# Three of six moves inside SBUF as ScalarE copies in place of DMA transfers, in a non-local attention block

## The reference

```
theta = x' w_theta' + b_theta          (N x Ci)
phi   = w_phi x + b_phi                (Ci x N)
g     = x' w_g' + b_g                  (N x Ci)
att   = softmax(theta phi, over the last axis)      (N x N)
y     = att g                          (N x Ci)
out   = w_out y + b_out, then batch norm by given mean, variance, gamma and beta
result = x + out
```

## Time and profile before

| what | value |
|---|---|
| median of three runs | 206.3 us (206.23 to 206.87) |
| the profiled execution | 205.01 us, of which 203.2 us are the span |
| TensorE's granted clock, as a share of full | 0.997 |
| PE, PEld (weight loads) busy | 195.2 us, 133.6 us |
| DVE, ACT, POOL busy | 174.8 us, 136.8 us, 154.2 us |
| DMA: bytes moved, hardware queue q1 | 35.28 MB, 81.3% of 16 engines' span |

### The profile page before, as it was taken

How to read it: one execution, slowest core, us unless ns; L and a number is a source line. 1 busy time by engine, 2 the same in 40 slices (tenths; PEclk the granted TensorE clock), 3 DMA queues, 4 the chain that set the end, 5 groups by cost and what they waited for, 6 DMA issues and landing times.

```text
span 203.2 us, 3990 instructions
## 1 busy us (share of the span) xinstructions
PE 195.2 (96%) x1100; PEld 133.6 (66%) x1100; DVE 174.8 (86%) x289; ACT 136.8 (67%) x245; POOL 154.2 (76%) x130
## 2 busy tenths in 40 slices
PE   7998899999999999999999999999999998999993
PEld 7485776587666857677566957677566956566551
DVE  0687989988997899978998899978998899989881
ACT  2679867767486766866577765866577675767731
POOL 2479579999778999699987999699988964954300
PEclk9999999999999999999999999999999999999998
DMA  5309946799999998899979998899988998848102
GB/s 154 98 7 225 240 85 117 167 248 185 188 219 250 222 169 221 187 224 187 233 159 259 230 191 194 168 249 203 198 180 182 226 169 182 132 81 155 52 3 103
DMA packets 59500, 35.28 MB, mean 174 GB/s; under 512 B 50400, under 2 KB 50912, under 8 KB 59488
## 3 DMA queue, kind: packets, MB, share of 16 engines
q1 hardware_dynamic: 59200, 35.01, 81.3%
q10 hardware_dynamic: 288, 0.14, 0.2%
HBM read 8.36 MB, written 4.23 MB: 62 GB/s over the span
## 4 chain that ended last, share of the span: by engine, by line
PE 71%; DVE 10%; DMA 5%; POOL 5%; SPq 4%; issue 3%; ACT 1%; ACTq 0%; DVEq 0%; POOLq 0%
PE ps_scores L757 21%; PE ps_flip L821 12%; PE ps_y L769 11%; PE ps_misc L783 6%; PE ps_y L776 5%; PE ps_misc L741 5%; DVE neg_max L622 4%; PE ps_misc L864 4%; DMA pt_hi<-p_hi 3%; DVE pt_lo L663 3%; SPq L302 2%; POOL p_lo L478 2%; DMA w_tp<-w_tp_t_dram 2%; PE ps_scores L795 1%; POOL x_lo L492 1%
## 5 line engine op out<-in xcount | busy, mean ns | idle before, releaser
L552 ACT ACTIVATE probs<-ps_scores,neg_max 128x1024 f32<-128x1024 f32 x64 | 71.7, 1120 | 29.1 <-DVE neg_max L627 14.9
L622 DVE TENSOR_REDUCE neg_max<-ps_scores 128x1 f32<-128x1024 f32 x64 | 77.9, 1217 | 9.5 <-PE ps_scores L757 9.1
L663 DVE SCALAR_TENSOR_TENSOR pt_lo<-ps_flip,pt_hi 128x512 f16<-128x512 f32 x84 | 54.0, 684 | 5.2 <-ACT pt_hi L539 5.1
L539 ACT ACTIVATE pt_hi<-ps_flip 128x512 f16<-128x512 f32 x84 | 45.6, 595 | 15.2 <-PE ps_flip L821 15.2
L478 POOL TENSOR_TENSOR p_lo<-probs,p_hi 128x1024 f16<-128x1024 f32 x22 | 47.0, 2139 | 4.7 <-POOL p_hi L471 3.9
L757 PE MATMUL ps_scores<-phi_hh,theta_hl 128*128 128x512 f32 x128 | 47.0, 448 | 0.8 <-ACT probs L552 0.6
L821 PE MATMUL ps_flip<-ident,probs 128*128 128x128 f32 x336 | 44.6, 275 | 1.8 <-DVE pt_lo L663 1.0
L821 PEld LDWEIGHTS ps_flip<-ident,probs 128*128 128x128 f32 x336 | 38.1, 142 | 11.1 <-issue 3.6
L757 PE MATMUL ps_scores<-phi_ll,theta_hl 128*128 128x512 f32 x128 | 40.1, 394 | 0.0
L769 PE MATMUL ps_y<-pt_hi,g_parts 128*128 128x512 f16 x120 | 28.4, 379 | 0.1
L757 PEld LDWEIGHTS ps_scores<-phi_ll,theta_hl 128*128 128x128 f32 x128 | 24.0, 188 | 5.6
(11 more groups left out here) (77 smaller groups left out, 173.8 us busy)
## 6 DMA issues: line engine op xcount, KB each, us to landing
x_in<-x_in_dram SPq DMA_DIRECT2D x16, 256.0 KB, 3.3
inv_all<-inv_row SPq DMA_DIRECT2D x15, 256.0 KB, 3.9
out_dram<-resid SPq DMA_DIRECT2D x15, 256.0 KB, 2.7
phi_hh<-hi SPq DMA_DIRECT2D x14, 256.0 KB, 5.7
phi_ll<-lo SPq DMA_DIRECT2D x14, 256.0 KB, 6.2
theta_hl<-hi SPq DMA_DIRECT2D x7, 256.0 KB, 4.7
theta_hl<-lo SPq DMA_DIRECT2D x7, 256.0 KB, 5.5
pt_hi<-p_hi SPq DMA_TRANSPOSE x22, 4.1
```

Of the source, the lines that this page charges most:

```text
L539: nc.scalar.activation(pt_hi[ring][:, c * HALF_TILES:(c + 1) * HALF_TILES, slot * P:(slot + 1) * P], ps_flip[c][:, :].rearrange("p (a n) - ...
L552: nc.scalar.activation(probs[k % PROB_RING][:, :], ps_scores[k % 2][:, :], ACT.Exp, bias=neg_max[:, k % STEPS:k % STEPS + 1], accum_out=ro ...
L622: nc.vector.tensor_reduce(out=top, in_=ps_scores[k % 2][:, :], op=ALU.max, axis=AX.X, negate=True).then_inc(row_max_ready if by_dma(it, k) ...
L663: nc.vector.scalar_tensor_tensor(out=pt_lo[ring][where], in0=ps_flip[c][:, :].rearrange("p (a n) -> p a n", n=P), scalar=PROB_SCALE, in1=p ...
```

## The change

Three of the six moves, those that keep their rows, are no longer transfers from SP but copies by ScalarE, from `hi` into `phi_hh` in step 3, from `lo` into `phi_ll` in step 6 and from `hi` into `theta_hl` in step 7 of the image before the one that uses them. Each copy is of 64 rows and 1024 columns, waits for GpSimd's signal, stands behind g's move and ahead of `pt_hi` and the exponential of its step, and counts up a new semaphore, `copied`. PE waits for that semaphore as well as for `stacked` ahead of the first scores of an image, and GpSimd ahead of writing `hi` anew. The number of transfers counted in `stacked` goes from six to three.

```diff
-    STACKS = 6
+    STACKS = 3
+    COPIES = 3
+    COPY_STEPS = (3, 6, 7)
...
                     sp.wait_ge(hi_ready, b + 1)
-                    restack(theta_hl[1 - r], 0, hi, 0, 1 - r)
                     restack(phi_hh[1 - r], 0, hi, CI, 1 - r)
-                    restack(phi_hh[1 - r], CI, hi, CI, 1 - r)
                     sp.wait_ge(lo_ready, 2 * b + 2)
                     restack(theta_hl[1 - r], CI, lo, 0, 1 - r)
                     restack(phi_ll[1 - r], 0, lo, CI, 1 - r)
-                    restack(phi_ll[1 - r], CI, lo, CI, 1 - r)
...
                         hold(stacked[r], it * 16 * STACKS + 16 * STACKS * ((k // MT + 1) // 2))
+                        hold(copied, COPIES * b)
...
+            def copy_rows(target, source, rows):
+                nc.scalar.activation(target[rows, :], source[rows, :].bitcast(F32), ACT.Copy).then_inc(copied, 1)
+
+            def same_rows(it, k):
+
+                image, j, ahead = image_at(it, k), k % MT, (k // MT + 1) % 2
+                if not exists(image + 1, B):
+                    return
+                if j == COPY_STEPS[0]:
+                    act.wait_ge(hi_ready, image + 1)
+                    copy_rows(phi_hh[ahead], hi, slice(CI, P))
+                if j == COPY_STEPS[1]:
+                    act.wait_ge(lo_ready, 2 * image + 2)
+                    copy_rows(phi_ll[ahead], lo, slice(CI, P))
+                if j == COPY_STEPS[2]:
+                    act.wait_ge(hi_ready, image + 1)
+                    copy_rows(theta_hl[ahead], hi, slice(0, CI))
...
                 if j == 0:
                     exponential(it, k)
+                same_rows(it, k)
                 high_parts(it, k)
                 if j != 0:
                     exponential(it, k)
...
                     pe.wait_ge(stacked[r], it * 16 * STACKS + 16 * STACKS * ((k // MT + 1) // 2))
+                    pe.wait_ge(copied, COPIES * image_at(it, k))
```

More of the change, by code:

```diff
@@ L148, in build_nonlocal_attention @@
         stacked = [sem(f"stacked{i}") for i in range(2)]
+        copied = sem("copied")
         stored = [sem(f"stored{i}") for i in range(2)]
```

## The result

The changed kernel takes 205.73 us (median of 22 runs, 205.17 to 206.56). The kernel before, run beside it, takes 204.64 us (median of 22, 203.74 to 208.50). The ratio is 1.005, 95% interval 1.0029 to 1.0070: slower by 0.6 to 1.4 us. The forecast was slower by 1.85 us, 208.15 us, range 206.6 to 209.3. Of the 2.4 us between 208.15 and 205.73, 1.66 come from the starting point (the three runs shown before had a median of 206.3) and 0.76 from the change.

A forecast was written before the change was run, and what follows sets the result against it. PE's matmuls were taken as the limit, with image 0 short of VectorE waiting for ScalarE. The terms 0.43 + 1.42 + 0 = 1.85 us, added to a median of 206.3, gave 208.15 us, range 206.6 to 209.3.

The forecast's parts named there:

- PE sets the pace from image 2 on, and the copies there are covered: Later images: PE is busy throughout, ScalarE's copies fit without delaying it; 0 in images 1 to 6.
- One copy costs 1.03 us: Each ScalarE copy of 64x1024 was put at 1.03 us, bounds 0.60 and 1.33.
- It occupies 0.94: A copy holds ScalarE some 0.94 us, since the next row starts about 0.1 before its predecessor ends.
- Image 0, step 3, 0.43: Copy into phi_hh ahead of tile 1's pt_hi delays PE's transposition of tile 2 by 0.43 us, bounds 0 and 0.73.
- Image 0, steps 6 and 7, 1.42: Copies into phi_ll and theta_hl delay PE's first scores of image 1 by 1.42 us, bounds 0.55 and 2.02.
- What reaches PE stays: no later gap exists to absorb it: In the full stretch read, 60 to 169 us, a delay that reaches PE is never won back.
- The removal of transfers, costed at 0: Dropping 21 transfers of 256 KB, three per image in seven images, gains nothing; bounds 0 and -1.7 us.
- given back, not slower: Rival, 12%: the freed queue lands pt_hi's transposes earlier, returning 1.7 us of PE's weight-load waits; 206.45 us.
- The starting point: The median of 206.3 us for the kernel before, to which the forecast's sum was added.

The follow-up runs named there:

- e6: The changed kernel with image 0's first copy in step 4 in place of step 3; median 205.06 us, 1.0034 of before.
- e12: The changed kernel run once more, unaltered, beside the kernel before; median 205.49 us, 1.0042 of before.
- e5: The changed kernel, but in image 0 the move of theta's hi stays a transfer issued by SP; median 205.51 us, 1.0053 of before.
- e9: e1 with VectorE's multiply of two columns of inv_sum split into two multiplies of one column; median 203.24 us, 0.9915 of before.
- e3: The changed kernel with the three replaced transfers issued all the same, into a spare tile, and waited for; median 206.63 us, 1.0094 of before.
- e10: The changed kernel with VectorE's two-column multiply of inv_sum split into two of one column; median 205.55 us, 1.0047 of before.
- e1: The changed kernel, but image 0's three moves stay transfers, copies only from image 1 on; median 203.66 us, 0.9917 of before.
- e4: The kernel before, with the three transfers left out from image 1 on and no copies instead; median 203.64 us, 0.9930 of before.
- e7: The kernel before, with the three row-keeping transfers issued by ScalarE instead of SP from image 1 on; median 204.66 us, 1.0041 of before.
- e8: e4 plus three transfers of 64 rows x 64 bytes issued by SP from image 1 on; median 204.27 us, 0.9972 of before.
- e11: e1 run once more, on the chip of e9 and e12; median 203.64 us, 0.9933 of before.

## Why the prediction was partly right and partly wrong

The place and the cause of the loss were right. What failed are the removal of the transfers, put at 0, the sentence that a delay of PE is never won back, and the median to which the sum was added. Image 0 was priced 0.6 us too low and about 1.9 us of gains were left out, so that the errors of the sum partly cancelled, which is luck.

- **PE sets the pace from image 2 on, and the copies there are covered: right, but for 0.18 us in image 4.** Images 2 to 6 are 0.17 us longer in all, with 0 forecast, and none waits for a copy. Most of it is image 4 (23.11 for 22.93), a price that the prediction did not have: VectorE's multiply is held longer by GpSimd there, and PE waits for VectorE.
- **One copy costs 1.03 us: right** (1.04 to 1.06). **It occupies 0.94: wrong.** 1.08 to 1.09, since nothing starts ahead of its end. In step 6 the copy also starts 0.12 later behind `g_raw` than `pt_hi` did, and the `pt_hi` behind it hands over 0.16 later.
- **Image 0, step 3, 0.43: mis-sized,** 0.54 by the gap and by e6 (0.74 and 0.79 in e12 and e5, where ScalarE first waits for `hi`).
- **Image 0, steps 6 and 7, 1.42: right in place and releaser, mis-sized,** 1.91. From `g_raw` to the exponential it is 1.36 more (2.81 for 1.45), where the sum had 0.94; the rest of the way is as computed, 2.25 for 2.20.
- **"What reaches PE stays: no later gap exists to absorb it": wrong for image 1.** The stretch that was read began at 60 us, behind image 1. There PE waited in all 0.8 us (23.76 for 22.97), little of it listed as PE's idle time, because modelled ends fill the gaps. About 0.5 came from VectorE and the transposing transfer that e9 shows, and lateness covers it (changed, e3, e6, e10 and e12 at 22.94 to 22.97; 23.47 to 23.51 in e1, e4, e5, e7, e8 and e11, none of them more than 1.8 late). The rest, some 0.28, went with the transfers. It stands in before at the sum behind this wait:
```profile
52.05 1.41 PEld L769 LDWEIGHTS ps_y<-pt_hi,g_parts 128*128 128x128 f16 x8 [0.93 <-DMA pt_hi<-p_hi]
```
- **The removal of transfers, costed at 0: wrong, and the main error of the sum.** Its bound of -1.7 us was the better figure: e4 measures -0.7 to -2.2 (e8, on another chip and with small transfers left in, -1.2 to +0.1). One execution was read, in which transfers were late in three places by little: of its 1.7 us of weight-load waits, the 0.28 in image 1 were PE's time, and images 2 and 3, which hold the other two, are within 0.03 us of e4's, which wait for none. In others with six transfers they are late by more: e3's transposing transfer took 8.39 us.
  The prediction also weighed a rule of the Trainium skill (Perfetto Trace Analysis, Identifying the Most-Contended Engine: matmul busy time is no good measure of nearness to the limit). From it and the row of waits it estimated -1.7 for this term, and e4's interval holds that. The room on PE that it inferred is not what the traces show: in a stretch without late transfers an image still takes 22.93 us, so PE has no room there; it is executions with late transfers that gain.
- **The rival "given back, not slower" had half of the mechanism at 12%, and wasn't combined with the forecast.** The transposing transfers do land earlier (a median of 3.2 us for 4.1), but the waits of one trace that it priced were not the price. The corrected sum: 2.43 (image 0) - 0.5 (image 1) + 0.2 (later images) - 1.4 (removal, by e4) = 0.7 us, against 0.6 to 1.4 measured. With e4's interval it is anything from -0.1 to 1.4, so the agreement is no close test.
- **The starting point.** The forecast of a time was added to a median of three runs of a kernel whose 22 runs have a median 1.66 us lower and reach from 203.74 to 208.50. The range allowed for the change's unknown costs, and for none in this. Alone it takes 208.15 to 206.49, just below the range; the sum's 0.76 alone would have left the time inside.

## What to carry to other kernels

A change that is covered in the steady loop can lose more than it gains in the first pass, where the order of work differs; here leaving image 0 out of it turned 1.004 into 0.993 on one chip (e12 and e11). When DMA engines are near full, as here at a share of 0.97 to 1.00, a transfer that nobody waits for can still make others land late: judge its removal by many runs and several traces, not by one trace's waits. And before a delay is called final, look for the next place where the delayed engine waits for another chain, in distances between starts rather than in listed idle time.

## What the runs showed of the hardware

- A VectorE multiply of 128x2 float32 took 0.17 to 0.18 us where no GpSimd operation ran or one ended within 0.16 us of its start. Where one went on for longer, in 59 cases in these traces, it took 0.29 to 1.72 us and ended 0.02 to 0.03 us behind that operation. A multiply of 128x1 took 0.14 to 0.16 us under any of them; two, 0.21 us for both. The Trainium skill (SBUF — State Buffer, SBUF: two separate sides) says that VectorE's two-port modes and GpSimd share a port pair, held by one for a whole instruction. The traces agree for the two-column form; that it runs in such a mode, and the one-column form does not, no run here shows.
- A ScalarE copy of 64x1024 float32 from SBUF takes 1.04 to 1.06 us, and in no trace did the next row start before its end. Rows out of PSUM were mostly followed up to 0.14 us before theirs, but not all: the `pt_hi` behind a copy was not.
- The start, up to the first transposition, took 16.07 to 18.84 us in the traces. In the profile of before PE's first projections had weight loads of 0.34 us until 6.4 us, in that of the changed kernel of 0.19 from 5.6 us on, at a granted clock that both show as 1.00. That is all of the 0.75 us between these two starts; its cause is open.
